# Sixteen-head attentions in 64x64 quarters, three PSUM bank pairs in turn, and stacks loaded in two halves

## The reference

```python
# layer 1: ALiBi                                # layer 2: rope on 8 channels, 4 key heads
att = (q @ k.T) / sqrt(8) + slope[h] * (j - i)   scores = (rope(q) @ rope(k).T) / sqrt(8)
# layer 3: 8 content + 32 rope channels per head
scores = (concat(qc, rope(qr)) @ concat(kc, rope(kr)).T) / sqrt(40)
# all three
att = softmax(where(j <= i, att, -inf)) ; y = (att @ v) @ W_out
```

## Time and profile before

| | us |
|---|---|
| median of three runs | 2904.51 (2901.69 to 2914.47) |
| the profiled execution, its own time | 2911.34 |
| its span, first to last instruction | 2909.5 |
| PE busy in the span | 2305.2 (79%) |
| DVE busy | 1535.6 (53%) |
| ACT busy | 1138.6 (39%) |

### The profile page before, as it was taken

The page is one execution under the profiler, slowest core; times in us unless marked ns, Lnnn a source line. Parts: engine busy times, 40 slices in busy tenths (PEclk is TensorE's granted clock), DMA queues, the critical chain, the costliest instruction groups (busy, mean ns, idle before and its releaser), DMA issues. The chain is left out here.

```text
span 2909.5 us, 54198 instructions
## 1 busy us (share of the span) xinstructions
PE 2305.2 (79%) x18107; PEld 1476.4 (51%) x18108; DVE 1535.6 (53%) x5386; ACT 1138.6 (39%) x1810; POOL 637.8 (22%) x689
## 2 busy tenths in 40 slices
PE   4487999997699999784888828447888866999997
PEld 1133777773267777431444416324554313777775
DVE  4635666635466665435677313147775245565663
ACT  5623554433244544333555402133554340233333
POOL 0204434300244342002010040421110012221210
PEclk8796999998899999896999869767999865899999
DMA  2000000000000000001222140202221002333330
GB/s 109 0 0 1 1 1 0 0 1 0 0 1 2 0 0 1 1 4 45 70 80 67 55 150 0 62 28 81 73 74 33 0 33 90 92 111 91 91 110 30
DMA packets 81241, 115.82 MB, mean 40 GB/s; under 512 B 10352, under 2 KB 67184, under 8 KB 77720
## 3 DMA queue, kind: packets, MB, share of 16 engines
q1 hardware_dynamic: 79024, 109.48, 12.4%
q0 software_dynamic: 2048, 4.20, 0.5%
HBM read 69.70 MB, written 42.86 MB: 39 GB/s over the span
## 5 line engine op out<-in xcount | busy, mean ns | idle before, releaser
L1240 ACT ACTIVATE at_pr<-ps 128x768 f32<-128x768 f32 x384 | 312.1, 813 | 505.7 <-PE ps L1176 505.7
L1282 DVE CUSTOM_DVE_ANT_0 at_junk<-ps,conf 128x128 f32<-128x128 f32 x768 | 220.1, 287 | 235.7 <-PE ps L1158 216.0
L1284 DVE CUSTOM_DVE_ANT_0 at_junk<-ps,conf 128x256 f32<-128x256 f32 x768 | 321.4, 419 | 0.0
L1158 PE MATMUL ps<-at_ks,at_qs 40*128 40x128 f32 (+5 forms) x2048 | 223.0, 321 | 70.7 <-DVE at_m L1284 26.9
L1170 PE MATMUL ps<-at_qs,at_ks 41*128 41x256 f32 (+5 forms) x2048 | 199.5, 294 | 58.2 <-DMA at_qs<-at_ml 28.4
L693 POOL TENSOR_TENSOR la_tc<-la_ta,la_tb 128x512 f32<-128x512 f32 x128 | 162.3, 1268 | 354.6 <-DVE la_tb L959 354.6
L710 PE MATMUL ps<-w_l0f,la_hs 128*128 128x512 f32 x256 | 152.5, 680 | 54.4 <-POOL la_hs L675 36.3
L1170 PEld LDWEIGHTS ps<-at_qs,at_ks 41*128 41x128 f32 (+2 forms) x2048 | 140.9, 145 | 105.9 <-ACT at_pr L1240 53.5
L860 ACT ACTIVATE la_pr<-ps 128x640 f32<-128x640 f32 x128 | 90.2, 705 | 265.8 <-PE ps L762 265.4
L1191 PE MATMUL ps<-at_pr,at_v 128*32 128x256 f32 (+1 forms) x3072 | 175.8, 341 | 16.4 <-issue 15.7
L1158 PEld LDWEIGHTS ps<-at_ks,at_qs 40*128 40x128 f32 (+2 forms) x2048 | 104.9, 151 | 160.3 <-DVE at_m L1284 59.2
(11 more groups left out here) (308 smaller groups left out, 4995.6 us busy)
## 6 DMA issues: line engine op xcount, KB each, us to landing
scratch_latent<-at_parts SPq DMA_DIRECT2D x32, 640.0 KB, 4.8
at_qs<-scratch_latent SPq DMA_DIRECT2D x32, 320.0 KB
at_ks<-scratch_latent SPq DMA_DIRECT2D x32, 320.0 KB
scratch_alibi<-at_parts SPq DMA_DIRECT2D x32, 192.0 KB, 2.3
at_ks<-scratch_alibi SPq DMA_DIRECT2D x192, 32.0 KB
scratch_rope<-at_parts SPq DMA_DIRECT2D x32, 192.0 KB, 2.3
at_ks<-scratch_rope SPq DMA_DIRECT2D x192, 32.0 KB
moe_weights<-in_moe SPq DMA_DIRECT2D x1, 4096.0 KB, 20.7
```

What stands on the lines that cost most here:

```text
L1158: m = nc.tensor.matmul(o[:, cols:cols + keys], q[:, block_q:block_q + P], kk[:, 0:keys], start=True, stop=True)
L1240: nc.scalar.activation(pr[:, p % RING, :, :], ps[:, 6:8, 0:384], ACT.Exp, scale=scale).then_inc(s.at_prob, 1)
L1282: nc.vector.tensor_tensor_reduce(junk[:, x % 2, e, 0:P], ps[:, m + e, 0:P], k.cf("late")[:, P:2 * P], 1.0, BIG, ALU.add, ALU.max, m2[:, r, ...
L1284: last_max = nc.vector.tensor_tensor_reduce(junk[:, x % 2, e, P:3 * P], ps[:, m + e, P:3 * P], k.cf("late"), 1.0, BIG, ALU.add, ALU.max, m ...
```

## The change

- `scores` and `keyed` are issued as 64x64 tiles: each product is split by output half `c` as well as by head `e`. The causal mask is added on TensorE to both of them (`quarter_masks`, four 64x64 products of 2x128 columns), for `c` != `e` from two new rolled constants. The constant `late` and the scratch `junk` go.
- VectorE's four custom instructions per pair become two plain `tensor_reduce` over both heads, which deliver the negated maximum.
- With split operands, banks 2 to 7 are three pairs used in turn by `keyed` and `scores` (`keyed_bank`, `score_bank`). In layer 3 the banks stay as they were. In each head step `keyed` now comes ahead of `scores`.
- The stacks are loaded in two halves of four pairs each, with a semaphore each (`at_stacked0`, `at_stacked1`); `scores` waits for the second at x = 4 only. Each half has as many DMAs as the whole had.
- Waits of `scores` and `keyed` sit on a `nop` of the sequencer. The row's extras move: transposed maxima to x = 0, value rows to x = 2, products to even x (except layer 2), `turn` and the division to x = 6, the copy of the attention out to ACT at x = 5; oT is copied by DVE, the output by ACT.

```diff
              ("local_q1", local_q1), ("local_k0", local_k0), ("sel", sel.reshape(P, -1))]
-    return parts
+    return parts + crossed
 
...
-        deep = 2 if split else 1
+        deep = split
+
+        def score_bank(n, x):
+            return 2 + 2 * ((n + 2 * x + 1) % 3) if deep else 2
+
+        def keyed_bank(n, x):
+            return 2 + 2 * ((n + 2 * x) % 3) if deep else 6
+
+        def until(i, x, first, back):
+            u = HP * i + x - first - back + 1
+            return HP * row0 + (min(max(u, 0), HP * B) if isinstance(i, int) else u)
+
+        def scored_until(i, x, back):
+            return until(i, x, 2 * HP, back)
+
+        def keyed_until(i, x, back):
+            return until(i, x, 3 * HP + KEY_LAG, back)
...
+            def load_half(i, n, g):
+                r, nr = i - 1, (n - 1) % slots
+                sem = (s.at_stacked0, s.at_stacked1)[g]
+                if g == 0:
+                    sp.wait_ge(s.at_scratch, 32 * (row0 + r + 1))
+                    sp.nop(nofuse=True)
+                at_least(sp, sem, 16 * (sd0 + nst * r))
+                sp.nop(nofuse=True)
+                if live(i, 1 + slots):
+                    at_least(sp, s.at_keyed, HP * (row0 + r - slots) + HP // 2 * (g + 1))
+                    sp.nop(nofuse=True)
+                for dst, src in a.stack_loads(nr, g):
+                    sp.dma_start(dst, src).then_inc(sem, 16)
...
+                    load_half(i, n, 0)
+                    load_half(i, n, 1)
...
+            def quarter_masks(bank, name):
+                for c in range(2):
+                    for e in range(2):
+                        r = slice(64 * e, 64 * e + 64)
+                        rows = k.cb(name if c == e else name + "_x")[r, :]
+                        out = ps[64 * c:64 * c + 64, bank + e, 0:3 * P].rearrange("p (b t) -> p b t", t=P)[:, 0:3:2, :]
+                        m = nc.tensor.matmul(out, k.cb("ident", 64 * e, 64)[r, :], rows.unsqueeze(1).to_broadcast([64, 2, P]),
+                                             start=False, stop=True, skip_group_check=True)
+                return m
+
...
             def scores(i, n, x):
-                u = HP * (row0 + i) + x
                 if x == 0:
-                    pe.wait_ge(s.at_stacked, 16 * (sd0 + nst * (i + 1)))
-                at_least(pe, s.at_max, u - deep + 1)
+                    pe.wait_ge(s.at_stacked0, 16 * (sd0 + nst * (i - 1)))
+                if x == HP // 2:
+                    pe.wait_ge(s.at_stacked1, 16 * (sd0 + nst * (i - 1)))
+                if deep:
+                    at_least(pe, s.at_prob, keyed_until(i, x, 1))
+                    if isinstance(i, int):
+                        at_least(pe, s.at_max, scored_until(i, x, 3))
+                else:
+                    at_least(pe, s.at_max, scored_until(i, x, 1))
+                pe.nop(nofuse=True)
+                bank = score_bank(n, x)
                 for block_q, cols, keys in ((0, 0, P), (P, P, 2 * P)):
-                    for e in range(2):
-                        q, kk = stacks(n, x, e, stack_rows)
-                        o = ps[:, 2 + 2 * (x % deep) + e, :]
-                        m = nc.tensor.matmul(o[:, cols:cols + keys], q[:, block_q:block_q + P], kk[:, 0:keys],
-                                             start=True, stop=True)
-                m.then_inc(s.at_score, 1)
+                    for c in range(2):
+                        for e in range(2):
+                            q, kk = stacks((n - 2) % slots, x, e, stack_rows)
+                            nc.tensor.matmul(ps[64 * c:64 * c + 64, bank + e, cols:cols + keys],
+                                             q[:, block_q + 64 * c:block_q + 64 * c + 64], kk[:, 0:keys],
+                                             start=(cols == 0), stop=False, skip_group_check=True)
+                quarter_masks(bank, "causal_q").then_inc(s.at_score, 1)
...
             def keyed(i, n, x):
-                u = HP * (row0 + i) + x
-                if x == 0:
-                    pe.wait_ge(s.at_mrow, 16 * (md0 + nm * (i + 1)))
-                at_least(pe, s.at_prob, u)
+                row, p = 3 + (x < KEY_LAG), (x - KEY_LAG) % HP
+                if p == 0:
+                    pe.wait_ge(s.at_mrow, 16 * (md0 + nm * (i - row + 1)))
+                if deep:
+                    at_least(pe, s.at_max, scored_until(i, x, 2))
+                    if isinstance(i, int):
+                        at_least(pe, s.at_prob, keyed_until(i, x, 3))
+                else:
+                    at_least(pe, s.at_prob, keyed_until(i, x, 1))
+                pe.nop(nofuse=True)
+                bank = keyed_bank(n, x)
                 for keys, cols, first in ((0, 0, 0), (P, 2 * P, P)):
-                    for e in range(2):
-                        q, kk = stacks(n, x, e, last)
-                        nc.tensor.matmul(ps[:, 6 + e, cols:cols + L - first], kk[:, keys:keys + P], q[:, first:L],
-                                         start=(cols == 0), stop=False, skip_group_check=True)
-
-            def keyed_masks():
-                for e in range(2):
-                    for cols in (0, 2 * P):
-                        m = nc.tensor.matmul(ps[:, 6 + e, cols:cols + P], k.cb("ident"), k.cb("causal_k"), start=False,
-                                             stop=(cols > 0), skip_group_check=True)
-                m.then_inc(s.at_keyed, 1)
...
             def step(i, n):
                 for x in range(HP):
+                    if live(i, 3 + (x < KEY_LAG)):
+                        keyed(i, n, x)
                     if live(i, 2):
-                        scores(i - 2, (n - 2) % slots, x)
-                    row = 3 + (x < KEY_LAG)
-                    if live(i, row):
-                        keyed(i - row, (n - row) % slots, (x - KEY_LAG) % HP)
-                        keyed_masks()
+                        scores(i, n, x)
                     if live(i, 5) and x == 0:
                         turn_back(i)
-                    if live(i, 3) and x == 1:
+                    if live(i, 3) and x == 0:
                         shifts(i, n)
                     if live(i, 5) and x == 2:
                         output(i)
-                    if live(i, 0) and x in product_at:
-                        product(i, n, product_at[x])
-                    if live(i, VALUE_ROW) and x == 5:
+                    if live(i, VALUE_ROW) and x == 2:
                         value_rows(i, (n - VALUE_ROW) % slots)
-                    if live(i, 4) and x == 7:
+                    for r in product_at.get(x, ()) if live(i, 0) else ():
+                        product(i, n, r)
+                    if live(i, 4) and x == 6:
                         turn(i)
...
-                        m = 2 + 2 * (x % deep)
-                        dve.nop(nofuse=True)
-                        for e in range(2):
-                            h = 8 * e + x
-                            nc.vector.tensor_tensor_reduce(junk[:, x % 2, e, 0:P], ps[:, m + e, 0:P], k.cf("late")[:, P:2 * P], 1.0, BIG,
-                                                           ALU.add, ALU.max, m2[:, r, 0, h:h + 1])
-                            last_max = nc.vector.tensor_tensor_reduce(junk[:, x % 2, e, P:3 * P], ps[:, m + e, P:3 * P], k.cf("late"), 1.0, BIG,
-                                                                      ALU.add, ALU.max, m2[:, r, 1, h:h + 1])
-                        last_max.then_inc(s.at_max, 1)
-                    if split and live(i, 3) and x == 1:
+                        at = score_bank(n, x)
+                        nc.vector.tensor_reduce(m2[:, r, 0, x:16:8], ps[:, at:at + 2, 0:128], AX.X, ALU.max, negate=True)
+                        nc.vector.tensor_reduce(m2[:, r, 1, x:16:8], ps[:, at:at + 2, 128:384], AX.X, ALU.max, negate=True
+                                                ).then_inc(s.at_max, 1)
+                    if split and live(i, 3) and x == 0:
...
+                        nc.vector.tensor_tensor(ml[:], ps[0:H16, 0, L:2 * L], mh[:], ALU.subtract).then_inc(s.at_mt, 1)
+                    if live(i, 5) and x == 0:
+                        dve.wait_ge(s.at_back, b - 4)
+                        at_least(dve, s.at_mt, row0 + done(i, 3))
+                        at_least(dve, s.at_out, b - 5)
+                        nc.vector.tensor_copy(oT[:], ps[:, 0, 0:L]).then_inc(s.at_turned, 1)
...
-    def stack_loads(n):
-        loads = []
+    def stack_loads(n, g):
+        loads, w = [], HP // 2 * L
         for e in range(2):
-            cols = slice(e * HP * L, (e + 1) * HP * L)
+            cols = slice((2 * e + g) * w, (2 * e + g + 1) * w)
             q, kk = (scr[n, j].rearrange("s (d h) t -> (s d) (h t)", h=H16)[:, cols] for j in range(2))
-            at = lambda stack, lo, hi: stack[64 * e + lo:64 * e + hi, n, :]
+            at = lambda stack, lo, hi: stack[64 * e + lo:64 * e + hi, n, g * w:(g + 1) * w]
...
```

(10 more changed lines are left out.)

134 lines of the change are left out of this document (66 added, 68 removed).

## The result

The changed kernel is slower: 2976.36 us median of four runs (2969.11 to 2987.88) against 2909.49 us for the kernel before (2901.69 to 2917.51). The ratio is 1.0227, 95% interval 1.019 to 1.0263. The forecast was 2915 us, and its range ended at 2948.

A forecast was written before the change was run, and what follows sets the result against it. It took TensorE to bound layer 3 and waits between engines layers 1 and 2. Terms of 21.5 + 3 - 2 - 12 = +10.5 us on 2904.5 us gave 2915 us, range 2880 to 2948.

The forecast's parts named there:

- main term: Layers 1 and 2: term 1, SyncE's queue becomes the bound, +21.5 us.
- term 1: SyncE's queue in layers 1 and 2: 18 more loads make rows 17.3 us; +21.5 us, bounds +7 and +35.
- term 5: Layer 3's loop back jump: VectorE's stalls go (-15.3), TensorE stalls instead (+13.4); together -2 us, bounds -15.3 and +8.
- SP has 5.2 us to spare: Layer 1, kernel before: SyncE's queue idles 5.2 us in a row of 15.7, taken as spare time.
- Term 4: Layer 3's row, bound by TensorE at 24.95 us: +0.25 us a row, +3 us over 13, bounds -8 and +11.
- Term 6: Layer 3's head: first scores start sooner with half loads (-4 us), clock rises sooner (-8 us); together -12 us.
- Terms 2 and 3: TensorE in layers 1 and 2: shorter steps hidden by SyncE (some 14.5 us rows without it); VectorE: hidden, nothing lost.
- The clock rival: Layers 1 and 2: waits at x = 4 halve TensorE's clock, +31 us on the forecast, 2945 us; chance 0.13.
- Products at 54 ns as a bound: All three layers: TensorE bound by its number of products, 54 ns each, 2934 us; chance 0.10.
- Half loads at half price: Layers 1 and 2: half loads cost half to issue, rows of 14.5 us, -52 us, 2850 or less; chance 0.05.

The follow-up runs named there:

- unroll: The changed kernel with TensorE's rows of layers 1 to 3 all written out, no back jump there: 2947.93 us, ratio 1.0132.
- before_half: The kernel before with every stack load issued as two DMAs of half the columns: 3138.87 us, ratio 1.0789.
- few_dmas: The changed kernel with parts stored already repeated in layers 1 and 2, so 8 loads a row instead of 36: 2889.14 us, ratio 0.9914.
- few_dmas_unroll: few_dmas with TensorE's rows of layers 1 to 3 written out: 2846.55 us, ratio 0.9773.
- before_unroll: The kernel before with the rows of layers 1 to 3 written out on TensorE and VectorE: 2899.39 us, ratio 0.9956.
- spread: few_dmas_unroll with products in single head steps, layer 3's at x = 2 to 6, layer 1's at x = 3: 2828.56 us, ratio 0.9706.
- spread_loop: spread with TensorE's loops back: 2860.34 us, ratio 0.9849.
- latent_dve_mask: whole_unroll with layer 3's score masks added by VectorE's four mask-and-maximum instructions instead of on TensorE: 2881.97 us, ratio 0.9882.
- no_quarters: whole_unroll with scores and keyed as products of 128 columns and their masks as full 128x128 products: 2940.84 us, ratio 1.0103.
- whole: The changed kernel with each row's stacks loaded whole again, 18 DMAs in layers 1 and 2: 2895.86 us, ratio 0.9942.
- whole_unroll: The changed kernel with stacks loaded whole and TensorE's rows of layers 1 to 3 written out: 2864.08 us, ratio 0.9844.

## Why the prediction was wrong

**The sign of the main term and its place were right; the size was not.** Layers 1 and 2 were to lose 21.5 us (bounds 7 and 35) and lost 58 in the profiled executions. Split at the copies of the maxima, their rows lost 64.8, the fills 6.2 (12 predicted), and the drains gave back 13.0 (12 predicted). So the failed step is the length of the row, 17.3 us predicted and 18.5 measured, on rows of 16.3 and 16.4. Two things make the difference, and a third reading was wrong without harm.
First, term 1 reckoned with clean issues: 9.7 us for the 24 DMAs of the row and 6.2 for 18 more make 15.9. In unroll, where no jump disturbs TensorE, nine rows between 1420 and 1600 us issue for 16.9 us each and pause for 1.6, and the layers still take 18.1 and 17.9 us a row. Single slow issues are the difference; the earlier trace rows already showed one of 1478 ns, and the sum ignored them. In before_half, with the same 42 DMAs in a row, issuing takes 16.1. What makes an issue slow I did not find.
Second, term 5 looked for the instruction fetch in layer 3 alone, though TensorE's body grows in all three loops. Unroll shows the stops of 4.2 to 4.4 us in layers 1 and 2 gone, and 15.7 us of the 58 with them (16.9 in the pair few_dmas and few_dmas_unroll).
Third, the idle time of the earlier trace rows was taken for slack. Before_half shows that it was part of a ring. For the changed kernel this error did no harm, as its scores start after the first half; the sentence "SP has 5.2 us to spare" was wrong all the same.

**Term 5, layer 3's jumps, -2 predicted, +12 to +18 found.** That VectorE's stalls go was right in kind and price (13.3 us in before_unroll's stretch of layer 3, 485.8 to 472.5, against 15.3). That TensorE stalls in their place was chosen rightly too, and q8 shows it. Its price, 13.4 us, was mis-sized: unroll measures 31.7 in layer 3, and few_dmas_unroll 25.7 against few_dmas. It varies from one execution to the next: spread and spread_loop are only 10.2 apart there. The sum had two stops at the jumps; the trace also has stops within the turns (0.85 to 1.47 us), and a lower clock after the ones looked at.
The Trainium skill, page "Runtime: NRT & Kernel Launch", section "Instruction fetch mechanics", led to the right side of that choice. By its figure of 2048 instructions, though, the bodies of layers 1 and 2 (1692 products and weight loads in three rows, some 1860 to 1900 with the waits, counted in the program) would have fitted; the trace shows 5 to 9 packets on q8 in each turn there and the longest stops of all, so the measurement decides against the figure as a threshold. The section also words the window that a target must lie in as two pages of 256 instructions; by that the body of before, some 1630, would have been fetched anew as well, and the earlier trace rows are against it.

**Term 4, layer 3's row, +0.25 us predicted, +1.35 found** (26.3 against 24.95, +17.5 us over 13 rows instead of +3, and beyond its bound of +11). The argument named the right place, odd x with little work, and judged it as nearly covered. Spread recovers 0.8 us a row of it, latent_dve_mask speaks against the second masks, and 0.55 stays open.

**Term 6, layer 3's head, -12 predicted.** From the first store to the first maxima, 49.7 us became 36.4: -13.3. The clock of its first two stretches is 0.81 and 0.73, where before it was 0.57 and 0.59. Right in sum, with some luck: few_dmas, with the same halves and products in layer 3, has 43.1 us there and a clock of 0.64, and whole, without the halves, 46.5 and 0.61, where the changed kernel has 36.4 and 0.77. So the gain of the halves alone is 3 to 10 us. The three terms make +22.6 if the jumps are taken from unroll and before_unroll, and 18.7 was measured. By the copies of the maxima the sum closes: -13.3 in the head, -1.9 in the first row, +16.2 in twelve full rows at 1.35, +15.5 for stops and jumps, +2.1 from there to the end.

**Terms 2 and 3** held. Quarters run side by side and the maxima are 1.03 us of DVE a step. But "hidden" has to be read with the bound: with SyncE relieved, the rows fall to 14.6 and 15.6 us (estimate 14.5), and no_quarters puts the worth of the quarters and their masks at 77 us.

**The rivals.** The clock rival, 2945, named a true effect. The clock between 1420 and 1600 us is 0.91 in unroll (waits of 28.3 us for the maxima, no jumps), 0.96 in whole (2.3 us of these waits, jumps), 1.00 in whole_unroll (0.4 us and no jumps) and 0.89 in the changed kernel with both, so the waits do lower it, as the rival said. Its price is not borne out: in unroll SyncE issues 16.9 of each 18.5 us, no pause of its queue there reaches 1.2 us, and it waits for nothing for more than 0.7 us in all, so slow steps of TensorE can have added little to these rows. Products at 54 ns as a bound are excluded: eight quarters of bf16 keyed and their four masks start within 0.30 us (1495.39 to 1495.69), 25 ns each. Half loads at half price are excluded by the 295 ns.

## What to carry to other kernels

Count what a queue issues in a row before cutting a transfer in two: here a load costs 0.3 us to issue with 16 KB, 32 KB or 320 KB in it, a load of 48 rows 0.33 to 0.47, a DMA of the maxima 0.64. The cure is a layout in which one DMA brings what several did, not fewer bytes. Idle time of a queue is slack only if nothing that it waits for waits for it in turn; lengthen it by one known amount and see whether the row grows by less. And when a change doubles an engine's instructions inside a hardware loop, look at the instruction queue in the second and third turn of every such loop, as a body that was fetched anew cost a stop at the jump here, in layer 3 stops within the turn as well, and a lower clock afterwards. Last, compare a profiled execution with its own median before a difference between two of them is given as a price.

## What the hardware showed that I had not expected

TensorE's stream stopped in the middle of a group of sixteen equal products (at 2720.7 us, for 1.47) in a looped body, but not in the same rows written out, though all of them are fetched too (34 packets in 270 us). In the loop of layer 1, bodies that are smaller than layer 3's stopped for longer (4.2 to 4.4 us against 2.8 to 2.9). I have no measurement that explains why the smaller body stops longer.
